# A fused two-layer transformer kernel in one program: projections as pairs of fp16 parts, the first queries by batch, weights split on the chip, and a new static order

## The reference

```python
xn = _layernorm(x, axis=-1)
x = x + _L0_attn_ref(xn, Wqkv, Wo) + _L0_ffn_ref(xn, A, B, Wr)
xn = _layernorm(x, axis=-1)
x = x + _L1_attn_ref(xn, Wq, bq, Wk, bk, Wv, bv) + _L1_ffn_ref(xn, gate_wq, gate_scale, up_wq, up_scale, down_wq, down_scale)
```

## Time and profile before

| | us |
|---|---|
| median of 3 runs | 666.8 |
| lowest and highest | 666.42 and 670.37 |
| the profiled execution | 666.2 |
| its span | 664.4 |
| TensorE busy | 620.2 (93%) |
| VectorE busy | 454.2 (68%) |
| ScalarE busy | 349.8 (53%) |
| GpSimd busy | 284.2 (43%) |

### The profile page before, as it was taken

One profiled execution on the slowest core, in us unless ns is written; L12 is line 12 of the kernel. 1 busy time (PEld: TensorE's weight loads), 2 busy tenths in 40 slices (PEclk: granted clock), 3 DMA queues, 4 the chain that ended last, 5 costly groups with the idle time before them and its releaser, 6 DMA issues.

```text
span 664.4 us, 11736 instructions
## 1 busy us (share of the span) xinstructions
PE 620.2 (93%) x4490; PEld 359.8 (54%) x4490; DVE 454.2 (68%) x936; ACT 349.8 (53%) x603; POOL 284.2 (43%) x299
## 2 busy tenths in 40 slices
PE   5989566978999999999999999999999999999997
PEld 4464444545665565565655755574654555454443
DVE  5775598984988987674668966686796554457422
ACT  3220696682558965843448748852684772023310
POOL 4203476550319773521315826632357561016310
PEclk9998685998999999999999999999999999999999
DMA  9364839466020400321103000401110000000001
GB/s 236 75 111 165 252 67 122 64 91 117 0 83 1 51 1 3 40 44 66 49 33 61 7 3 1 51 33 35 33 33 1 1 1 33 33 33 0 1 16 48
DMA packets 34567, 34.78 MB, mean 52 GB/s; under 512 B 8816, under 2 KB 24080, under 8 KB 34512
## 3 DMA queue, kind: packets, MB, share of 16 engines
q1 hardware_dynamic: 27424, 23.36, 16.6%
q0 software_dynamic: 2672, 8.36, 6.5%
q10 hardware_dynamic: 4416, 2.31, 1.3%
HBM read 30.15 MB, written 8.39 MB: 58 GB/s over the span
## 4 chain that ended last, share of the span: by engine, by line
PE 78%; DVE 8%; ACT 5%; issue 4%; DMA 3%; SPq 1%; POOL 0%; ACTq 0%; DVEq 0%
PE B_bank L1014 28%; PE B_bank L1035 14%; PE A_bank L983 10%; PE A_bank L900 5%; PE B_bank L922 5%; PE A_bank L954 4%; PE E_bank L938 3%; ACT probs L810 2%; DVE mx L1225 2%; ACT e L809 2%; PE A_bank L869 2%; PE B_bank L900 2%; PE E_bank L934 2%; DMA q_parts<-qs 1%; PE B_bank L1004 1%
## 5 line engine op out<-in xcount | busy, mean ns | idle before, releaser
L733 POOL TENSOR_TENSOR probs<-e,probs 128x512 f16<-128x512 f32 x128 | 153.8, 1208 | 189.4 <-ACT probs L810 179.7
L1014 PE MATMUL B_bank<-xs,wgu 128*128 128x512 f16 x896 | 200.5, 379 | 0.0
L809 ACT ACTIVATE e<-E_bank,wn 128x512 f32<-128x512 f32 x192 | 135.6, 706 | 100.1 <-PE E_bank L938 52.5
L1014 PEld LDWEIGHTS B_bank<-xs,wgu 128*128 128x128 f16 x896 | 85.4, 98 | 96.3
L810 ACT ACTIVATE probs<-E_bank,wn 128x512 f16<-128x512 f32 x192 | 135.6, 706 | 0.0
L1035 PE MATMUL B_bank<-wd,hbuf 128*128 128x512 f16 x448 | 100.3, 379 | 0.0
L1225 DVE TENSOR_REDUCE mx<-B_bank 128x8 f32<-128x256 f32 (+6 forms) x168 | 87.5, 584 | 7.2 <-PE B_bank L922 7.1
L745 POOL TENSOR_TENSOR hbuf<-hf,hbuf 128x512 f16<-128x512 f32 x56 | 67.7, 1215 | 43.7 <-ACT hbuf L836 43.6
L983 PE MATMUL A_bank<-wo_sb,attnT 128*128 128x512 f32 x160 | 71.1, 594 | 0.0
L922 PE MATMUL B_bank<-kk,qq 128*128 128x32 f16 (+20 forms) x512 | 67.4, 269 | 3.5 <-DVE mx L1225 3.2
L1035 PEld LDWEIGHTS B_bank<-wd,hbuf 128*128 128x128 f16 x448 | 43.4, 98 | 48.3
(11 more groups left out here) (155 smaller groups left out, 626.0 us busy)
## 6 DMA issues: line engine op xcount, KB each, us to landing
qq<-q_parts SPq DMA_DIRECT2D x21, 256.0 KB
x<-in_x SPq DMA_DIRECT2D x20, 256.0 KB, 4.3
out_y<-x SPq DMA_DIRECT2D x16, 256.0 KB, 2.0
xa<-in_x SPq DMA_DIRECT2D x12, 256.0 KB, 4.9
q_parts<-qs SPq DMA_DIRECT2D x12, 256.0 KB, 3.3
wgu<-in_gate_w POOLq DMA_DIRECT2D x4, 448.0 KB, 5.3
wgu<-in_up_w POOLq DMA_DIRECT2D x4, 448.0 KB, 5.1
wd<-in_down_w POOLq DMA_DIRECT2D x4, 448.0 KB, 7.6
```

The costliest lines, as they stand in the source:

```text
L733: pool.tensor_tensor(probs[:, u % PSLOTS, 1, :], e32[:, w, :], probs[:, u % PSLOTS, 0, :], ALU.subtract).then_inc(s_lo01, 1)
L809: act.activation(e32[:, w, :], psum("exp", i, g, w)[:, :], ACT.Exp, scale=wn[:, 7:8])
L1014: mm = pe.matmul(psum(name, c, i)[:, :].rearrange("p (t n) -> p t n", t=NT), wgu[:, m, k, i * P:(i + 1) * P], xs[:, :, part, k, :], start= ...
```

## The change

- **fp16 pairs.** For chunks 1 to 3, `xT0` leaves a pair: ScalarE writes the high fp16 part times 256, VectorE the low part (new step `xT0` on DVE, which now frees the bank). `tok` and `q` use weights that are pairs too, `wtok2` and `wq2`, with three products per block: high x high, high x low, low x high (`PAIRS`). `q` becomes two steps, `qa` and `q`, of 6 matmuls. Chunk 0 keeps fp32.
- **The output product.** `attT` on ScalarE writes the high part of the turned attention, VectorE the low part and frees the bank. The low-rank middle is one turned fp16 tile that holds its high and low part in 128 rows (`midT`). `outa` and `out` are 6 and 8 fp16 matmuls. The scale that undoes the weights' factor is applied where VectorE adds the input.
- **Weights.** Scaled fp16 high parts by ScalarE (`hi`, 10 steps of two activations, one with four), low parts by GpSimd (`lo`, 10 subtractions). The fp32 originals lie in `hbuf`. Further sums of squares and norms (`squares2`, `norm2`, `scale2`) give the factors; the one of Wo waits for its load. The `order` has `lo` 0 to 4 ahead of the first exp unit, 5 to 9 between exp units.
- **First q by batch.** Chunk 0's q is computed for batch 0 in four tiles of 256 columns, then for batch 1 (`q0`), with a store each, so that the first gather waits for batch 0 alone.
- **Moves.** Four of the eight `hot` copies become one DMA of 1 MB by SyncE; `setup2` moves from VectorE to GpSimd; `half` and `down` are cut into four steps with the same matmuls over the same 512 tokens; `late` and `ffn_load` may start earlier; all of `US` and `RANK` is new.

The diff, cut to its core:

```diff
+PAIRS = ((0, 0), (0, 1), (1, 0))
...
-        "pv": (14, 1), "attT": (34, 1), "out": (14.5, -2), "xT1": (7, 0), ...
+        "norm2": (-124, 3), "qa": (125.5, -1, -11), "q": (-65, 4), "max": (-47, 3, -6), "exp": (36, 3, -169), ...
...
-        p.add("POOL", ("ffn_load", n), pool("late", 10), at=74.0 + 7.0 * n)
+        p.add("POOL", ("ffn_load", n), pool("late", 4), sp("gather", 1, gap=8.0), at=40.0 + 5.0 * n)
...
+            def lo(n):
+                pool.wait_ge(s_whi, n + 1)
...
+                pool.tensor_tensor(low, scaled, high, ALU.subtract).then_inc(s_wlo, 1)
...
+            def squares2(n):
...
+                    act.wait_ge(s_wo, 48)
...
+            def hi(n):
+                act.wait_ge(s_sw, 1) if n < NK else act.wait_ge(s_scale2, 1 if n == NK else 2)
+                if n < NK:
+                    act.activation(wq2[:, n, 0, :], wq_sb[:, n, :], ACT.Identity, scale=wm[:, 15:16])
+                    last = act.activation(wq_scaled[:, n, :], wq_sb[:, n, :], ACT.Identity, scale=wm[:, 15:16])
...
+            def store(b, m):
+                wait_used(act, "q0", b, m)
+                act.dma_start(q_dram[0, m * P:(m + 1) * P, :, b, :], qs[:, m % 2, :, b * SEQ:(b + 1) * SEQ]).then_inc(s_q0[b][m], 16)
...
+            def q_tiles(c, m, ks):
+                for k in ks:
+                    for n, (wpart, xpart) in enumerate(PAIRS):
+                        mm = pe.matmul(psum("q", c, m)[:, :].rearrange("p (t n) -> p t n", t=NT), wq2[:, k, wpart, m * P:(m + 1) * P],
+                                       xp[:, :, xpart, k, :], start=(k == 0 and n == 0), stop=(k == NK - 1 and n == 2))
...
+            def out_tiles(i, t, ks):
+                for k in ks:
+                    for n, (apart, wpart) in enumerate(PAIRS if k < NK else PAIRS[0:2]):
...
-                for k in range(NK + 1):
-                    mm = pe.matmul(psum("out", i, t)[:, :], attnT[:, k, t * P:(t + 1) * P], wo_sb[:, k, :],
-                                   start=(k == 0), stop=(k == NK))
...
+            def xT0(c, t):
+                dve.wait_ge(s_xTh, NT * (c - 1) + t + 1)
+                dve.scalar_tensor_tensor(out=xp[:, t, 1, :, :].rearrange("p k n -> p (k n)"), in0=psum("xT0", c, t)[:, :], scalar=XS,
+                                         in1=xp[:, t, 0, :, :].rearrange("p k n -> p (k n)"), op0=ALU.mult,
+                                         op1=ALU.subtract).then_inc(free("xT0", c, t), 1)
```

533 lines of the change are left out of this document (361 added, 172 removed), and 12 rows, old and new, of tables (RANK, US).

## The result

| | before | predicted | after |
|---|---|---|---|
| median of the runs, us | 667.3 | 628.0 (613 to 643) | 647.0 (645.7 to 647.9) |
| ratio to before | 1 | 0.941 | 0.969 (0.966 to 0.973) |
| profiled span, us | 664.4 | 626.9 | 646.0 |
| first maxima, TensorE | 44.5 | 40 to 41 | 48.6 |
| row of maxima issued | 57.3 | 54.5 | 67.4 |

The kernel is 3% faster, so the direction was right, and 19 us slower than the forecast, outside its range. The two parts came out differently. From the first gate block on 20.8 us were gained where 17.5 were forecast. Ahead of it nothing was: 2.4 us were lost where 20 should have been won. These 22.4 us, less the 3.3 of the first part, are the 19.1 us of the miss.

A forecast was written before the change was run, and what follows sets the result against it. TensorE was taken as the bound from the first gate block on, and before it whichever wait ends last. 664.4 - 17.5 (gate block on) - 20 (start) + 1.8 = 628.7, given as 628 us, range 613 to 643.

The forecast's parts named there:

- Part A: From the first gate block (190.6 us) on: 19.5 us saved, less 2 of new TensorE waits, 17.5 us gained.
- The rival of VectorE as the bound of pool A: VectorE's bank releases hold TensorE: 28 releases at 2.4 us would cost 67 us, giving 695 us; chance 0.04.
- step 1: First gather, needing only batch 0's stores: maxima begin at 40 to 41 us, 4 us earlier.
- Step 2: Batch 0's maxima: their row is ready at 54.5 us against 57.3, 3 us earlier, if step 3 allows it.
- step 3: New start wait, TensorE's norm of Wo behind its load: just in time; with the longer library wait 4 us late.
- step 4: Between maxima and exp, `tok` and seven `max` groups replace 10.93 us of q: first exp at 61 us against 66.0.
- step 5: GpSimd's library wait leaves its first exp operation: ScalarE's fourth unit can start at about 64.5 us, 11.5 us earlier.
- step 6: Batch 0: its rest takes 29 us against 24, a 3.77 us wait goes; batch 1 starts at 93.5, 10 us earlier.
- step 7: Batch 1: VectorE loses set-up work and gets six low parts; 1 us of gain, between -3 and 3.
- step 8: Batch 1 to the first gate block: smaller matmuls and a store wait gone; 9 us gain, at least 4.
- The rival built on it (642.7 us): TensorE stands at the norm of Wo, 8 us or more late; the start gains only 6 us: 642.7 us; chance 0.17.
- The upper rival: The load of Wo holds the start, the same rival as the 642.7 us one; chance 0.17.

The follow-up runs named there:

- Experiment 8: The changed kernel with only the high x high product of every `out`, 5 matmuls instead of 14: 635.33 us.
- experiment 1: The changed kernel with the hot rows copied by VectorE again instead of the 1 MB DMA: 642.18 us, ratio 0.962.
- experiment 18: The program of experiment 1 run once more, unchanged: 640.94 us, ratio 0.959.
- experiment 2: The changed kernel with the squares and norm of Wo moved behind the first exp units: 649.40 us.
- experiment 4: The changed kernel with hot rows by VectorE, the norm of Wo behind the first exp units, and the first four `wgu` loads behind the small loads: 640.69 us.
- experiment 13: The kernel of experiment 9 with the first four `wgu` loads issued behind the row's transfer and the small loads: 641.90 us.
- experiment 16: The vector row without Wo parts 5 to 9, with narrower VectorE low parts, `dsb` scaling on GpSimd, all-reduce on TensorE, later `wgu` loads: 636.43 us.
- experiment 10: The kernel before the change with a one-column GpSimd addition right behind its partition_all_reduce: 662.97 us against 667.08, ratio 0.993.
- experiment 9: The vector row with GpSimd's partition_all_reduce replaced by a TensorE multiplication and a VectorE maximum: 642.30 us.
- the vector row: The kernel of experiment 1, the changed kernel with hot rows copied by VectorE: 642.18 us, and 640.94 us in experiment 18.
- experiment 15: The kernel of experiment 13 with the second layer's small loads and set-up steps moved earlier, out of batch 0: 642.46 us.
- experiment 12: The vector row without low parts 5 to 9 of Wo on GpSimd and high parts 5 to 9 on ScalarE: 642.30 us.
- experiment 5: The vector row with the last scaling of `dsb` moved from VectorE to GpSimd: 640.96 us.
- experiment 6: The vector row with `hi` and `lo` 5 to 8 of Wo moved from batch 0 to batch 1: 643.40 us.
- experiment 11: The vector row without the low parts 5 to 9 of Wo on GpSimd: 641.15 us.
- experiment 14: The vector row with 7.5 us of VectorE's low parts in batches 0 and 1 made narrow: 641.72 us.
- experiment 17: The vector row with all-reduce on TensorE, later `wgu` loads, `dsb` scaling on GpSimd, and Wo parts 5 to 8 in batch 1: 641.42 us.
- experiment 7: The vector row with GpSimd's partition_all_reduce moved behind the issue of the load of Wo: 645.61 us.

## Why the prediction was right, and why it was wrong

**Part A, right.** 20.8 us for 17.5. Each term was on: `out`, q and VectorE's 285 us as worked out, `tok` at the lower bound, and the new waits cost 0.6 us of TensorE (7.9 less 7.3) instead of 2. Turning the middle in fp16, which was set to zero, took 0.9 us of TensorE away. Experiment 8 adds what the text did not have: behind TensorE the next bound was close. The rival of VectorE as the bound of pool A did not come, but together with ScalarE it stands some 8 us further on.

**Where the 22.4 us went.** Against the forecast the first maxima were 8.1 us late (step 1), their row 4.8 more (steps 2 and 3), the first exp matmul 0.9 more (step 4), the fourth unit 1.5 more (step 5), the first exp matmul of batch 1 6.3 more (step 6) and the first gate block 0.8 more (steps 7 and 8).

**Step 1, wrong in sign, the largest miss (8.1 us).** It counted the stores, ScalarE's `hi` and the gathers' issues, and gave the 1 MB DMA for the hot rows no line at all. The transfer held up 8 issues of SyncE behind it and ScalarE's stores, 5 to 6 us that stay to the end (experiments 1 and 18). With it removed the step is late by 2 to 3 us.

**Step 2** counted 14 us from the first maxima to their row. It was 18.8, 4.0 of them TensorE's wait for the norm of Wo, which belongs to step 3. With the norm moved away it was 15.1 and 16.9 (experiments 2 and 4), 1 to 3 us more than counted.

**Step 3, right in mechanism, its size too small.** It named the wait for the norm of Wo and the library wait ahead of it, "just in time; with the longer library wait it is 4 us late". TensorE waited 4.0 us, and the load landed 11.5 us after its issue and not 6, with the gather of batch 1 in flight beside it. The rival built on it (642.7 us) is 4 us from the time, and that by luck: moving the norm away (experiment 2) returned nothing.

**Step 4** had the order right: `tok` and seven groups stand there. The row's transfer ends last instead, 6.8 us; only experiments 4, 13 and 16, with the `wgu` loads behind it, came near 61, at 64.6 to 65.6.

**Step 5, right in mechanism.** The wait left the first exp unit: from the first exp matmul to the fourth unit there are 5.0 us instead of 10.0 (3.5 forecast). By itself the move is worth 4 us of the kernel before (experiment 10). In the changed kernel the wait stands ahead of the load of Wo; taking it away there altogether (experiment 9) gave no time.

**Step 6, wrong, and the only one whose cause stays open.** It counted 29 us from the fourth unit to the first exp matmul of batch 1; it took 35.3 (27.7 before). It listed TensorE's q, ScalarE's four `hi` and GpSimd's new work, added no price for `hi` to ScalarE's 21 units, and gave VectorE no new work at all, although the low parts of chunk 1's q and the set-up of the second layer came into this stretch: from the fourth to the 25th unit VectorE's busy time went from 24.9 to 34.5 us (95%), ScalarE's from 25.2 to 32.2, GpSimd's from 22.5 to 29.9. The standing of VectorE behind GpSimd's runs was there only as 5 us over both batches; one operation alone stood for 3.7.

The omitted work does not act by its amount, though. The changed kernel needs 36.5 us between these units, the vector row 36.7 and 36.8; with 5.8 us of VectorE gone (experiment 15) it was 36.2, with the parts of Wo left out (12) 34.8. From the first exp to the gate, experiments 5, 6, 11, 12, 14 and 16, in which up to 19 us of work were moved or removed, took 116.5 to 118.9 us, the vector row itself 117.1 and 116.2, the changed kernel 118.1, where 109.5 were forecast; only against the kernels that also began early by later `wgu` loads (4, 13 and 17, 120.6 to 122.1) is 16 shorter. The reading that fits the runs is a ring: each exp unit waits for an `e` slot that VectorE or GpSimd frees, each `pv` for both, each of their lists has other work in a fixed order, and relief of one engine is waited away at the next. Shown is that no single engine's amount of work is the bound, and that relief of three together gives 3 to 5 us; the ring itself is argued, and why batch 0 takes 6.3 us more than counted stays open. What would shorten the ring, fewer steps in it or another order of the lists, was not tried.

**Steps 7 and 8, right in sum and in part by luck.** From batch 1 to the gate 77.0 us were forecast and 77.8 measured. But step 7 expected 1 us of gain, at most 3, and up to batch 1's last unit 5.4 came, with VectorE 3.5 us less busy; step 8 expected 9 us, at least 4, and from that unit to the gate 4.0 came. ScalarE's wait of 6.39 us for the store of a q tile is gone, as forecast.

Of the prediction's own signs of being wrong three came: TensorE waited 4.0 us at `norm2` and 4.4 us before a `pv`, and the first gate block was at 192.9.

The upper rival took the start's steps as waits of which one goes wrong. What happened was three at once (the hot transfer, the load of Wo, the row's transfer) and a batch 0 that is longer than counted and that hardly any relief shortens, and that was in no rival.

## What to carry to other kernels

A change of the start is priced by what becomes of it at the last milestone before the bound part, not at the first unit: here 4 to 5 us won at the first exp unit (experiments 4 and 13, against 1 and 9) left nothing clear of the scatter at the gate, while 5 to 6 us were kept where they came from ahead of everything (the 1 MB transfer) and 4 where a wait went in a stretch with idle engines (the touch of experiment 10). Where work moves between stages, list it for every engine in the stage that it enters, not only in the one that it leaves. Price every DMA that a change adds by its bytes and by what is issued in the 10 us behind it, on all queues. And touch GpSimd's ordinary code once, right behind a library instruction, where it is idle.

## What the runs showed of the hardware that was not expected

- Around a `partition_all_reduce` there are two waits with nothing in the profile to wait for: 5.3 to 5.9 us ahead of the instruction and 6.7 to 9.5 before the next ordinary operation in all kernels that have it, but 8.9 and 11.2 us in the one run with the load of Wo and the gather of batch 1 beside them (experiment 7). Both go when the instruction goes (experiment 9).
- VectorE's SBUF operations stand through several back-to-back GpSimd subtractions, not one, and end in the first gap: 0.48 us became 4.14 behind three and 3.04 behind two, 0.29 became 3.55 behind three.
- A 1 MB transfer between SBUF rows made other issues of the same engine 3.6 times as long (1.82 to 6.57 us).
- A row of 32 KB was read 4.2 us after its issue with nothing large issued just ahead of it, and 9.0 us after it beside four loads of 448 KB (experiments 13 and 9).
